# Maxima of the attention scores as two operand rows instead of a product of their own, another order of the lap, and zero fills moved one stage ahead

## The chip, the cores and the metric

One NeuronCore of a Trainium2 chip runs the whole program. The metric is the device time of one execution in microseconds; a profile is taken of one execution. PE is TensorE, DVE VectorE, ACT ScalarE, POOL GpSimd, SP the engine that here only issues DMAs. PE's granted clock is given as a share of 2.4 GHz.

## The reference

Two layers run over x of 32 sequences with 128 tokens of 128 channels. Each has a conditioning part and an expert part with eight experts, of which each token takes two. The change lies in the second layer's attention (16 heads, 8 channels each) and in the last steps of the first layer's experts:

```
q, k, v = split(layernorm(x) @ w_qkv + b_qkv)       # 16 heads of 8 channels
scores  = einsum('bqhd,bkhd->bhqk', q, k) / sqrt(8)
attn    = softmax(scores, axis=-1)                  # exp(score - maximum) / sum
x       = x + einsum('bhqk,bkhd->bqhd', attn, v) @ w_o + b_o
h       = layernorm(x)                              # then routing and experts
```

## The kernel before

The program is a row of stages, each a block in which all engines start together: layer 0 with its dispatch (to 106 us), its experts (`experts0`, to 237), conditioning and the q, k and v products (`pre_attention`, to 306), attention with norm, routing and dispatch of its result (`attention`, to 542), the second experts (`experts1`).

**Attention.** A lap `s` of 46 serves one sequence at each step of a software pipeline; four heads form a group g, 0 to 3. q and k are kept as a high and a low part, so that a product has 96 rows. PE computes the scores twice. `score(s + 2, g)` gives them with queries on the partitions, in ps1, against `km`, a k masked for each head by POOL (one head of four, `mask_k`) and ACT (three). From these DVE takes the negative maximum of each query (`maximum`, L1735, into `mneg`). `shift(s, g)` gives them with keys on the partitions, in ps2, against `qm`, a q masked by SP's loads from DRAM (`load_masked`, twelve DMAs for a pair of sequences), and adds the maxima; ACT then takes the exponent straight from ps2 (`exponent`, L1833). To bring the maxima into that layout POOL parts them into a high and a low piece (`part_max`, L1680 and L1682), PE turns them (`turn_max`, L1902), DVE spreads them over four masked blocks (`spread_max`, L1741, into `mxT`), and a second product with `selr` adds them in ps2 (L1896). ps1 and ps2 have two halves each, so a score waits for the maximum of two groups before, and a shift for the exponent of two groups before.

`mix` (L1914) multiplies the exponents with `vb`, the values spread by POOL (`spread_v`, L1690), `total` (L1923) sums them; DVE inverts and divides (`invert`, `divide`), `project` (L1933) applies w_o, and `keep` (L1756) adds the result to X3. From lap 6 on the group of four sequences that is done gets its norm, routing and dispatch in pieces, spread over four laps: moments and variance (lap 6), centring and turning (7), scaling and natural rows (8), routing (9), placing (10), where POOL also sends two pieces of rows in each lap (`post_scatter`, L358). In the text lap A is a lap with moments and placing, B the one with centring and turning, C with scaling, D with routing; they repeat.

The order is written out by hand for each engine. On PE a lap is four times score, shift, with `mix` behind the shift of g 0, `turn_max(s + 1)` behind that of g 1 (or 2), `project` behind that of g 2 (or 3), `total` behind that of g 3. SP loads the next pair's q and k (`load_pair`, three DMAs of 128 KB each), then the masked q, and in two pairs a fill.

**Fills.** The rows that experts read are written in the dispatch; regions of zeros are written before (`fill_region`, two DMAs of 1040 KB for each expert). Six of the eight regions of the second dispatch are filled in layer 0, two in attention. POOL waits for them in lap 10.

**End of the first experts.** SP loads rows and weights of each tile, then the modulations `eg` (L1007), then calls `fetch_halves`: V in four DMAs when the first sends are done, X3 in four when the second are (L865). DVE adds V to X (L956, needs all four), then two groups of X3 (L964), and the stage ends.

## Time and profile before

| | us |
|---|---|
| median of three runs (lowest, highest) | 696.9 (695.83, 698.49) |
| profiled execution: its time, its span | 700.72, 698.9 |
| PE, DVE, POOL, ACT busy, share of the span | 85%, 68%, 62%, 56% |
| mean granted clock of PE | 0.929 |

Starts of stages are read from the timeline, in us from the span's start. A duration of a matmul overlaps with the next one's, so what it costs in a row of such is the distance of two starts. A busy time by stretch counts overlapped parts once.

### The profile page before, as it was taken

To read this page: it belongs to the slowest core of one execution; us is meant where nothing else is said; L and a number is where in the kernel's file an instruction comes from. 1 tells how busy PE (TensorE), PEld (TensorE's weight loads), DVE (VectorE), ACT (ScalarE), POOL (GpSimd) and SP (SyncE) were. 2 spreads that over 40 slices of the span, in tenths; PEclk is the share of its full clock that TensorE was granted. 3 is DMA by queue.
4 is the path that set the end of the run, shared out by engine and by line. 5 is a ranking of instruction groups with operands and counts; after the bars stand their busy time and mean duration, and the time that the engine had idled before them with its cause. 6 is when DMAs were issued, how large, how long until landed. Compare 5 with 4: busy or idle time off the path is not lost.

```text
span 698.9 us, 17755 instructions
## 1 busy us (share of the span) xinstructions
PE 593.7 (85%) x5559; PEld 475.7 (68%) x5559; DVE 473.7 (68%) x1514; ACT 389.3 (56%) x841; POOL 433.3 (62%) x573
## 2 busy tenths in 40 slices
PE   4999953999998378869999999999961699999996
PEld 2566632988998256536766766766741599999993
DVE  3665552766777367756878788879745478888874
ACT  3544401655555068776777777778641355555551
POOL 2677760666677565534454878977777155666663
PEclk9999995999999589967999999999985699999999
DMA  7999996767677518561873443443113798888858
GB/s 224 249 203 297 288 260 145 196 205 198 202 224 226 202 39 247 205 203 55 251 202 87 111 125 105 127 126 85 47 36 98 220 300 269 251 249 252 246 186 267
DMA packets 106298, 131.23 MB, mean 188 GB/s; under 512 B 16272, under 2 KB 83888, under 8 KB 106096
## 3 DMA queue, kind: packets, MB, share of 16 engines
q1 hardware_dynamic: 92864, 109.40, 57.1%
q0 software_dynamic: 9088, 18.76, 8.2%
q10 hardware_dynamic: 4272, 2.14, 1.0%
q8 instruction: 39, 0.64, 0.4%
q14 instruction: 35, 0.29, 0.1%
HBM read 80.75 MB, written 49.50 MB: 186 GB/s over the span
## 4 chain that ended last, share of the span: by engine, by line
PE 29%; POOL 12%; issue 9%; DVE 2%; DMA 2%; ACT 1%; SPq 1%; ACTq 0%; POOLq 0%; DVEq 0%
PE psO L2058 10%; PE psA L939 8%; POOL late_rows L358 7%; PE ps L1884 2%; PE ps L1894 2%; PE ps L1896 2%; POOL vb L1690 2%; PE psAO L1914 2%; PE psAO L1923 1%; PE psT L889 1%; POOL X L1480 1%; POOL rstd L1473 1%; DMA kp<-qk_parts 1%; POOL xmx L1682 1%; SPq L1129 1%
## 5 line engine op out<-in xcount | busy, mean ns | idle before, releaser
L948 POOL DMA_INDIRECT expert_rows<-fo,to x78 | 84.6, 1085 | 62.5 <-DVE fo L2081 49.1
L1735 DVE TENSOR_REDUCE mneg<-ps 128x4 f32<-128x512 f32 x128 | 86.2, 676 | 41.4 <-PE ps L1884 39.9
L948 POOL DMA_INDIRECT expert_rows<-eo,to x78 | 75.1, 962 | 53.9 <-ACT eo L1094 34.2
L1833 ACT ACTIVATE arena<-ps 128x512 f32<-128x512 f32 x128 | 75.5, 590 | 49.8 <-PE ps L1896 48.8
L358 POOL DMA_INDIRECT dispatch_rows<-row,index x64 | 62.4, 976 | 34.4 <-issue 19.2
L921 DVE CAST xh<-psT 128x256 fp32r<-128x256 f32 x78 | 33.1, 424 | 66.6 <-PE psT L889 65.9
L358 POOL DMA_INDIRECT late_rows<-row,index x64 | 63.9, 998 | 20.3 <-issue 15.1
L939 PE MATMUL psA<-xh,wh 128*128 128x256 f32 (+1 forms) x234 | 73.3, 313 | 1.4 <-DVE xl L925 1.4
L1826 ACT ACTIVATE km<-kp,const 96x512 fp32r<-96x512 f32 x96 | 67.7, 712 | 3.4 <-PE ps L1884 1.3
L1884 PE MATMUL ps<-km,qp 96*128 96x512 f32 x128 | 63.4, 502 | 4.8 <-ACT km L1826 3.6
L939 PE MATMUL psA<-xh,wl 128*128 128x256 f32 (+1 forms) x234 | 66.9, 286 | 0.0
L939 PE MATMUL psA<-xl,wh 128*128 128x256 f32 (+1 forms) x234 | 66.7, 285 | 0.0
L1670 POOL TENSOR_SCALAR km<-kp,const 96x512 fp32r<-96x512 f32 x32 | 50.1, 1565 | 15.1 <-POOLq L1180 10.2
L2058 PE MATMUL psO<-wb,fh 128*128 128x128 f32 x464 | 56.4, 275 | 0.3 <-ACT fh L2140 0.3
L2058 PEld LDWEIGHTS psO<-wb,fh 128*128 128x128 f32 x464 | 54.3, 192 | 0.5 <-ACT fh L2140 0.5
L1894 PE MATMUL ps<-qm,kp 96*128 96x512 f32 x128 | 52.6, 411 | 0.9 <-DVE mxT L1741 0.5
L1896 PE MATMUL ps<-mxT,selr 128*128 128x512 f32 x128 | 51.7, 404 | 0.0
L939 PEld LDWEIGHTS psA<-xh,wh 128*128 128x128 f32 (+1 forms) x234 | 42.7, 182 | 2.3 <-DVE xl L925 2.2
L939 PEld LDWEIGHTS psA<-xl,wh 128*128 128x128 f32 (+1 forms) x234 | 42.8, 183 | 0.0
L939 PEld LDWEIGHTS psA<-xh,wl 128*128 128x128 f32 (+1 forms) x234 | 42.6, 182 | 0.0
L1884 PEld LDWEIGHTS ps<-km,qp 96*128 96x128 f32 x128 | 25.6, 201 | 19.4 <-issue 11.5
L2129 ACT ACTIVATE fw<-psO,xt 128x128 f32<-128x128 f32 x58 | 18.2, 365 | 33.7 <-PE psO L2058 27.2
(232 smaller groups left out, 1570.6 us busy)
## 6 DMA issues: line engine op xcount, KB each, us to landing
late_rows<-tail SPq DMA_DIRECT2D x17, 1040.0 KB, 18.4
wb<-in_W1b SPq DMA_DIRECT2D x29, 578.0 KB
w<-in_W SPq DMA_DIRECT2D x29, 304.0 KB
qk_parts<-qk SPq DMA_DIRECT2D x8, 1024.0 KB, 4.7
qp<-qk_parts SPq DMA_DIRECT2D x48, 128.0 KB
kp<-qk_parts SPq DMA_DIRECT2D x48, 128.0 KB
qm<-qk_parts SPq DMA_DIRECT2D x192, 32.0 KB
arena<-in_W1b SPq DMA_DIRECT2D x10, 578.0 KB
```

Source lines behind the costliest of these rows:

```text
L358: pool.indirect_dma_start(out=r.xbuf, out_offset=bass.IndirectOffsetOnAxis(ap=r.index[b][:, c:c + 1], axis=0), in_=r.row[b][:, c // TOPK, ...
L921: v.tensor_copy(z.xh[q][:], z.psT[:, q, 0:SLOTS]).then_inc(z.x_high, 1)
L939: ins = z.m.nc.tensor.matmul(out, w[k][q][:, columns], x[k][q][:], start=(k == 0), stop=(k == 2), skip_group_check=True)
L948: pool.indirect_dma_start(out=m.ybuf, out_offset=bass.IndirectOffsetOnAxis(ap=to[b][:, a:a + 1], axis=0), in_=out[b][:, a, :], in_offset=N ...
L1670: ins = nc.gpsimd.tensor_scalar(km[s % 2][:, :, j, :], kp[side(s)][:, :, tok(s)].bitcast(F32), mask(j), None, ALU.mult)
L1735: nc.vector.tensor_reduce(mneg[s % 2][:, g, :], ps1[:, g % 2, :].rearrange("p (j k) -> p j k", j=4), AX_X, ALU.max, negate=True).then_inc( ...
L1826: nc.scalar.activation(km[s % 2][:, :, j, :], kp[side(s)][:, :, tok(s)].bitcast(F32), ACT.Copy, scale=mask(j)).then_inc(km_act, 1)
L1833: nc.scalar.activation(prob[s % 2][:, g, :], ps2[:, g % 2, :], ACT.Exp, scale=ATT_SCALE).then_inc(exped, 1)
L1884: nc.tensor.matmul(ps1[:, g % 2, :], qp[side(s)][:, g, tok(s)], km[s % 2][:, g].rearrange("p j k -> p (j k)"), start=True, stop=True).then ...
L1894: nc.tensor.matmul(ps2[:, g % 2, :].rearrange("p (j k) -> p j k", j=4), kp[side(s)][:, g, tok(s)], qm[(s // 2) % 2][:, g, :, tok(s)], star ...
L1896: nc.tensor.matmul(ps2[:, g % 2, :], selr[:, g, :], mxT[s % 2][:].rearrange("p j k -> p (j k)"), start=False, stop=True).then_inc(shifted, 1)
L2058: ins = nc.tensor.matmul(psO[:, q, a * P:(a + 1) * P], h[q][:, k, a * P:(a + 1) * P], wb[b][:, WIDE + k * P:WIDE + (k + 1) * P], start=(k ...
```

## The change

The two pieces of the maxima become rows 96 and 97 of `qm`, against two rows of ones in `kp`, so that one product of 98 rows gives the shifted scores; L1896, `selr` and the spreading go. `mneg` is turned as it is (`turn_max` waits for DVE, not POOL), DVE parts the turned maxima with a copy and a subtraction (16 partitions, 128 columns), and SP sends each piece into its row of `qm` with a DMA of 8 KB (`send_max`); the shift waits for both (`max_landed`). `part_max` goes from POOL. The turned maxima and `project`'s result now lie in free columns of psAO instead of psM and psW, and the waits that guarded those two go. On PE `turn_max` stands at the head of the lap, `mix` behind the shift of g 1, `project` ahead of `total`; DVE's order follows. SP's list is written anew: k of pair k + 1, nine masked loads, the maxima of the even sequence, the last three masked loads, q of pair k + 2. The last two regions are filled in `experts0`, between `eg` and `fetch_halves`. In the diff the leading blanks of attention's lines are cut.

```diff
@@ -1006,6 +1004,8 @@
...
                         [DOWN, GT, 2 * P])).then_inc(m.gbu_in[b], 16)
+                for e in range(EARLY_FILLS, E):
+                    fill_region(m, sp, e)
                 fetch_halves(m, sp, st, 0)
...
@@ -1119,12 +1119,15 @@
...
+MAX_ROW = 96
...
-def load_pair(m, sp, n, b):
...
-    for side, parts in ((m.qp[b], (0, 1, 0)), (m.kp[b], (2, 2, 3))):
+def load_pair(m, sp, n, b, sides="qk"):
...
+    for name, side, parts in (("q", m.qp[b], (0, 1, 0)), ("k", m.kp[b], (2, 2, 3))):
+        if name not in sides:
+            continue
...
@@ -1229,7 +1232,7 @@
...
-                    nc.gpsimd.memset(m.qm[b][:].bitcast(F32), 0.0).then_inc(m.zeroed, 1)
+                    nc.gpsimd.memset(m.qm[b][0:MAX_ROW].bitcast(F32), 0.0).then_inc(m.zeroed, 1)
...
@@ -1575,11 +1578,12 @@
...
-    m.qp, m.kp = ([m.sb(f"{x}{b}", [96, HG, PAIR], F32R, ctx) for b in range(PAIR_BUFFERS)]
-                  for x in ("qp", "kp"))
+    m.qp = [m.sb(f"qp{b}", [96, HG, PAIR], F32R, ctx) for b in range(PAIR_BUFFERS)]
+    m.kp = [m.sb(f"kp{b}", [MAX_ROW + 2, HG, PAIR], F32R, ctx) for b in range(PAIR_BUFFERS)]
...
-    m.qm = [m.sb(f"qm{b}", [96, HG, 4, PAIR], F32R, ctx) for b in range(2)]
+    m.qm = [m.sb(f"qm{b}", [MAX_ROW + 2, HG, 4, PAIR], F32R, ctx) for b in range(2)]
...
+    m.max_in = m.sems("a_max_in0", "a_max_in1")
...
@@ -1594,11 +1598,31 @@
...
+def send_max(m, sp, s, rows, ready, shifted):
...
+    to, half = m.qm[(s // 2) % 2], slice((s % 2) * P, (s % 2 + 1) * P)
+    if s >= 4:
+        sp.wait_ge(shifted, HG * (s - 3))
+    for w in range(2):
+        sp.wait_ge(ready, 2 * s + w + 1)
+        sp.dma_start(to[MAX_ROW + w:MAX_ROW + w + 1, :, :, half].rearrange("o g j k -> o (g j) k").bitcast(F32),
+                     rows[:, w, :].bitcast(F32)).then_inc(m.max_in[s % 2], 16)
...
+def max_landed(engine, m, s):
...
+    engine.wait_ge(m.max_in[s % 2], 32 * (s // 2 + 1))
...
+MAXIMA, BY_WO = slice(2 * P, 3 * P), slice(3 * P, 4 * P)
...
@@ -1608,23 +1632,22 @@
...
-        selr = sb("selr", [P, HG, P], F32R)
...
-        xm = two("xmx", [P, 4, HG, 2])
-        mxT = two("mxT", [P, 4, P], F32R)
+        mxT = two("mxT", [HEADS, 2, P], F32R)
...
-        (cleared, made, km_pool, km_act, vb_done, scored, maxed, link, parted, turned, mxT_done, shifted,
+        cleared = m.zeroed
+        (made, km_pool, km_act, vb_done, scored, maxed, turned, mxT_done, shifted,
...
-            "a_cleared", "a_made", "a_km_pool", "a_km_act", "a_vb", "a_scored", "a_maxed", "a_link", "a_parted",
+            "a_made", "a_km_pool", "a_km_act", "a_vb", "a_scored", "a_maxed",
...
@@ -1642,19 +1665,26 @@
...
 def _(sp):
-    for k in range(PAIRS):
-        ahead = k + 1
-        if 2 <= ahead < PAIRS:
-            if ahead >= PAIR_BUFFERS:
-                sp.wait_ge(shifted, HG * 2 * (ahead - PAIR_BUFFERS + 1))
-            if ahead % 2 == 0:
-                sp.wait_ge(m.qk_out[ahead // 2 % 2], 16 * (ahead // 4 + 1))
-            load_pair(m, sp, ahead, ahead % PAIR_BUFFERS)
+    sp.wait_ge(m.qk_out[1], 16)
+    load_pair(m, sp, 2, 2)
+    send_max(m, sp, 0, mxT[0], mxT_done, shifted)
+    for k in range(1, PAIRS):
+        send_max(m, sp, 2 * k - 1, mxT[1], mxT_done, shifted)
+        if PAIR_BUFFERS <= k + 1 < PAIRS:
+            sp.wait_ge(shifted, HG * 2 * (k + 2 - PAIR_BUFFERS))
+            load_pair(m, sp, k + 1, (k + 1) % PAIR_BUFFERS, "k")
         if k >= 2:
             sp.wait_ge(shifted, HG * 2 * (k - 1))
-            load_masked(m, sp, k)
-        if k in (2, 3):
-            fill_region(m, sp, EARLY_FILLS + k - 2)
+            load_masked(m, sp, k, range(3))
+        send_max(m, sp, 2 * k, mxT[0], mxT_done, shifted)
+        if k >= 2:
+            load_masked(m, sp, k, (3,))
+        if k + 2 < PAIRS:
+            sp.wait_ge(scored, HG * 2 * (k + 3 - PAIR_BUFFERS))
+            if k % 2 == 0:
+                sp.wait_ge(m.qk_out[(k + 2) // 2 % 2], 16 * ((k + 2) // 4 + 1))
+            load_pair(m, sp, k + 2, (k + 2) % PAIR_BUFFERS, "q")
+    send_max(m, sp, SEQS - 1, mxT[1], mxT_done, shifted)
     sp.wait_ge(mixed, SEQS)
...
@@ -1667,19 +1697,9 @@
...
-            ins = nc.gpsimd.tensor_scalar(km[s % 2][:, :, j, :], kp[side(s)][:, :, tok(s)].bitcast(F32),
+            ins = nc.gpsimd.tensor_scalar(km[s % 2][:, :, j, :], kp[side(s)][0:96, :, tok(s)].bitcast(F32),
...
-    def part_max(s):
-        p = s % 2
-        pool.wait_ge(maxed, HG * (s + 1))
-        wait(pool, turned, s - 1)
-        hi, lo = (xm[p][:, :, :, w] for w in range(2))
-        mine = mneg[p][:].rearrange("p g j -> p j g")
-        nc.gpsimd.tensor_copy(hi.bitcast(F32R), mine).then_inc(link, 1)
-        pool.wait_ge(link, s + 1)
-        nc.gpsimd.tensor_tensor(lo, mine, hi, ALU.subtract).then_inc(parted, 1)
...
@@ -1693,10 +1713,6 @@
...
-        ins = nc.gpsimd.memset(mxT[b][:].rearrange("p j k -> p (j k)").bitcast(F32), 0.0)
-    ins.then_inc(cleared, 1)
-    part_max(0)
-    for b in range(2):
...
@@ -1704,8 +1720,6 @@
...
-        if s + 1 < SEQS:
-            part_max(s + 1)
...
@@ -1730,39 +1744,41 @@
...
-            wait(dve, parted, s - 1)
+            wait(dve, turned, s - 1)
...
-        wait(dve, shifted, HG * (s - 1))
-        nc.vector.tensor_tensor(mxT[s % 2][0:32], bc(psM[0:32, 0:P].unsqueeze(1), 32, 4, P),
-                                bc(m.const[0:32, C_MASK:C_MASK + 4].unsqueeze(2), 32, 4, P),
-                                ALU.mult).then_inc(mxT_done, 1)
+        if s >= 2:
+            max_landed(dve, m, s - 2)
+        hi, lo = (mxT[s % 2][:, w, :] for w in range(2))
+        mine = psO[0:HEADS, s % 2 ^ 1, MAXIMA]
+        nc.vector.tensor_copy(hi, mine).then_inc(mxT_done, 1)
+        dve.wait_ge(mxT_done, 2 * s + 1)
+        nc.vector.tensor_tensor(lo, mine, hi.bitcast(F32), ALU.subtract).then_inc(mxT_done, 1)
...
-        dve.wait_ge(made, s + 1)
+        dve.wait_ge(made, s + 2)
...
-        nc.vector.tensor_tensor(m.X3[:, s, :], psW[:, 0:P], m.X3[:, s, :], ALU.add).then_inc(kept, 1)
...
-    for g in range(HG):
-        ins = nc.vector.tensor_copy(selr[:, g, :], bc(m.const[:, C_SEL + g:C_SEL + g + 1], P, P))
-    ins.then_inc(cleared, 1)
+        nc.vector.tensor_tensor(m.X3[:, s, :], psO[:, s % 2, BY_WO], m.X3[:, s, :], ALU.add).then_inc(kept, 1)
...
+    for b in range(PAIR_BUFFERS):
+        ins = nc.vector.memset(kp[b][MAX_ROW:MAX_ROW + 2].bitcast(F32), 1.0)
+    ins.then_inc(made, 1)
...
-        if g == 2:
-            dve.wait_ge(cleared, 2)
+        if g == 1:
...
@@ -1770,36 +1786,35 @@
...
         varying, centring, routing, placing = (group(s, k) for k in (6, 7, 9, 10))
+        if s + 1 < SEQS:
+            spread_max(s + 1)
         if s + 2 < SEQS:
             maximum(s + 2, 0)
-        if varying is not None:
-            post_moments(post, dve, varying, kept)
         if centring is not None:
...
             post_logits(post, dve, routing, routing % 2, post.natural_banks)
+        if s + 2 < SEQS:
+            maximum(s + 2, 1)
         if inner:
             invert(s - 2)
-        if s + 2 < SEQS:
-            maximum(s + 2, 1)
+            divide(s - 2)
         if varying is not None:
-            post_gather(post, dve, varying)
+            post_moments(post, dve, varying, kept)
         if placing is not None:
             index_slot(r, dve, placing, post.rank_out)
-        if inner:
-            divide(s - 2)
         if routing is not None:
...
             maximum(s + 2, 2)
+        if varying is not None:
+            post_gather(post, dve, varying)
         if varying is not None:
...
             index_place(r, dve, placing, post.rank_out)
-        if s + 1 < SEQS:
-            spread_max(s + 1)
         if s + 2 < SEQS:
...
@@ -1889,17 +1904,14 @@
...
                 pe.wait_ge(qm_in[(s // 2) % 2], 16 * 12 * (s // 4 + 1))
-            pe.wait_ge(mxT_done, s + 1)
+            max_landed(pe, m, s)
         wait(pe, exped, HG * s + g - 1)
         nc.tensor.matmul(ps2[:, g % 2, :].rearrange("p (j k) -> p j k", j=4), kp[side(s)][:, g, tok(s)],
-                         qm[(s // 2) % 2][:, g, :, tok(s)], start=True, stop=False)
-        nc.tensor.matmul(ps2[:, g % 2, :], selr[:, g, :], mxT[s % 2][:].rearrange("p j k -> p (j k)"), start=False, stop=True
-                         ).then_inc(shifted, 1)
+                         qm[(s // 2) % 2][:, g, :, tok(s)], start=True, stop=True).then_inc(shifted, 1)
...
     def turn_max(s):
-        pe.wait_ge(parted, s + 1)
-        wait(pe, mxT_done, s)
-        nc.tensor.transpose(psM[0:32, 0:P], xm[s % 2][:].rearrange("p j g w -> p (j g w)"), m.ident
+        pe.wait_ge(maxed, HG * (s + 1))
+        nc.tensor.transpose(psO[0:HEADS, s % 2 ^ 1, MAXIMA], mneg[s % 2][:].rearrange("p g j -> p (g j)"), m.ident
                             ).then_inc(turned, 1)
...
@@ -1908,7 +1920,7 @@
...
-            wait(pe, divided, s - 1)
+            wait(pe, kept, s - 1)
...
@@ -1929,58 +1941,43 @@
...
         pe.wait_ge(divided, s + 1)
-        wait(pe, kept, s)
-        nc.tensor.matmul(psW[:, 0:P], oT[s % 2][:], m.wo[:], start=True, stop=True).then_inc(projected, 1)
+        nc.tensor.matmul(psO[:, s % 2, BY_WO], oT[s % 2][:], m.wo[:], start=True, stop=True).then_inc(projected, 1)
...
     score(1, 0)
+    turn_max(0)
     score(1, 1)
-    turn_max(0)
     score(1, 2)
-    pe.wait_ge(cleared, 3)
+    score(1, 3)
+    pe.wait_ge(made, 1)
     shift(0, 0)
-    score(1, 3)
     shift(0, 1)
...
         turning, scaling, routing, placing = (group(s, k) for k in (7, 8, 9, 10))
+        if s + 1 < SEQS:
+            turn_max(s + 1)
         for g in range(HG):
...
                 shift(s, g)
-            if behind and g == 0:
+            if behind and g == 1:
                 mix(s - 1, range(4))
+            if g == 3 and inner:
+                project(s - 2)
             if behind and g == 3:
...
             if g == 0 and placing is not None:
-                wait(pe, kept, min(s - 2, SEQS))
                 pe.wait_ge(post.nat_copied, placing + 1)
...
                 post_rank(post, pe, placing, placing % 2, post.rank_out)
-            if g == (1 if routing is None else 2) and s + 1 < SEQS:
-                if scaling is not None:
-                    pe.wait_ge(post.hT_done, scaling + 1)
-                if routing is not None:
-                    pe.wait_ge(post.nat_copied, routing + 1)
-                    pe.wait_ge(post.router.got, routing + 1)
-                turn_max(s + 1)
-            if g == (2 if routing is None and placing is None else 3) and inner:
-                if routing is not None:
-                    pe.wait_ge(post.nat_copied, routing + 1)
-                    pe.wait_ge(post.router.got, routing + 1)
-                if placing is not None:
-                    pe.wait_ge(post.router.slotted, placing + 1)
-                project(s - 2)
         if turning is not None:
-            wait(pe, mxT_done, min(s + 2, SEQS))
             wait(pe, post.nat_copied, turning)
...
         if scaling is not None:
-            wait(pe, kept, min(s - 1, SEQS))
-            wait(pe, mxT_done, min(s + 2, SEQS))
             wait(pe, post.router.slotted, scaling)
...
```

## Rows read from the trace of the kernel before

**Rows 1.** Busy time by stretch: length, then each engine's busy us (instructions), granted clock, DMA share, GB/s
```profile
314.26:322.56 8.30, 8.02 (x18) 4.84 (x18) 5.08 (x8) 4.46 (x8) 4.88 (x11) 0.50 0.01 2
322.56:502.25 179.69, 172.46 (x2432) 123.85 (x2431) 143.26 (x436) 134.91 (x254) 126.64 (x253) 1.00 0.47 128
```

**Rows 2.** Busy time of one lap without later work, columns as above
```profile
345.30:350.87 5.57, 5.57 (x80) 3.93 (x80) 4.45 (x9) 4.10 (x7) 3.33 (x8) 1.00 0.91 276
```

**Rows 3.** Timeline of PE: start, us, engine, line, out<-in, count
```profile
329.95 0.40 PE L1894 MATMUL ps<-qm,kp 96*128 96x512 f32 x1
330.19 0.40 PE L1896 MATMUL ps<-mxT,selr 128*128 128x512 f32 x1
330.42 0.27 PE L1902 MATMUL psM<-const,xmx 128*32 128x128 f32 x1
```

**Rows 4.** Busy time of one cycle of four laps
```profile
426.67:451.94 25.27, 24.02 (x343) 17.38 (x343) 20.62 (x70) 19.40 (x37) 20.86 (x39) 1.00 0.40 115
```

**Rows 5.** Timeline of PE; in brackets the idle time before and what ended it
```profile
314.26 0.76 PE L1894 MATMUL ps<-qm,kp 96*128 96x512 f32 x1 [0.48 <-DVE mxT L1741]
...
322.56 1.68 PE L1914 MATMUL psAO<-arena,vb 128*32 128x128 f32 x32
...
328.60 1.08 PE L1914 MATMUL psAO<-arena,vb 128*32 128x128 f32 x32
...
410.54 0.28 PE L1902 MATMUL psM<-const,xmx 128*32 128x128 f32 x1 [1.25 <-POOL xmx L1682]
```

**Rows 6.** Timeline of DVE at the end of the first expert stage
```profile
230.45 4.91 DVE L956 TENSOR_TENSOR X<-V,X 128x512 f32<-128x512 f32 x8 [2.93 <-DMA V<-expert_rows]
```

**Rows 7.** Part 6 of the page, DMA issues: KB each, median us to landing
```profile
late_rows<-tail SPq DMA_DIRECT2D x17, 1040.0 KB, 18.4
```

**Rows 8.** Timeline of SP's queue: start of the first issue, us until the last is issued
```profile
215.12 0.92 SPq L1007 DMA_DIRECT2D eg<-cond_rows  x2
...
412.47 1.69 SPq L1129 DMA_DIRECT2D qp<-qk_parts  x3
...
415.62 4.14 SPq L1594 DMA_DIRECT2D qm<-qk_parts  x12
```

**Rows 9.** Timeline of POOL, the mask of k in lap 7
```profile
359.34 1.57 POOL L1670 TENSOR_SCALAR km<-kp,const 96x512 fp32r<-96x512 f32 x1 [3.01 <-DMA kp<-qk_parts]
```

**Rows 10.** The chain of work that ended last, in order of time
```profile
353.41 5.84 DMA kp<-qk_parts
```

**Rows 11.** Busy time by stretch, columns as in rows 1
```profile
216.00:230.50 14.50, 9.87 (x83) 9.36 (x82) 8.83 (x24) 5.91 (x15) 11.14 (x12) 0.92 0.74 243
...
334.00:344.00 10.00, 10.00 (x149) 7.18 (x151) 8.59 (x16) 7.44 (x14) 4.17 (x12) 1.00 1.03 294
336.00:340.00 4.00, 4.00 (x57) 2.79 (x58) 3.17 (x7) 2.88 (x6) 1.43 (x3) 1.00 1.07 341
```

**Rows 12.** Timeline of POOL at the border of laps A and B
```profile
407.60 1.09 POOL L358 DMA_INDIRECT late_rows<-row,index  x1 [0.99 <-DVE index L339]
...
409.96 0.21 POOL L1680 CAST xmx<-mneg 128x16 fp32r<-128x16 f32 x1
...
410.47 1.57 POOL L1670 TENSOR_SCALAR km<-kp,const 96x512 fp32r<-96x512 f32 x1
```

**Rows 13.** Timeline of DVE: first maxima of laps B, D and A, and two others
```profile
407.24 0.27 DVE L1756 TENSOR_TENSOR X<-psW,X 128x128 f32<-128x128 f32 x1
407.43 0.67 DVE L1735 TENSOR_REDUCE mneg<-ps 128x4 f32<-128x512 f32 x1
...
420.83 0.69 DVE L1735 TENSOR_REDUCE mneg<-ps 128x4 f32<-128x512 f32 x1 [1.75 <-PE ps L1884]
...
424.90 0.66 DVE L1741 TENSOR_TENSOR mxT<-psM,const 32x512 fp32r<-32x512 f32 x1
...
426.67 0.67 DVE L1735 TENSOR_REDUCE mneg<-ps 128x4 f32<-128x512 f32 x1
```

**Rows 14.** DMA issues: KB each, us to landing
```profile
condT<-in_condT SPq DMA_DIRECT2D x1, 8.0 KB, 1.9
```

6 lines of the change are left out of this document (2 added, 4 removed).

## Prediction

> **What bounds the kernel now.** I read the busy times by stretch first. The attention stage from its second lap to the last scoring lap takes 179.69 us, and PE is busy for 172.46 of them at a granted clock of 1.00; before it stand 8.30 us at 0.50 [rows 1]. A lap is one sequence of 32. In the laps without later work PE has no gap: 5.57 us busy out of 5.57, DVE 4.45, ACT 4.10 [rows 2]. Each of the four maxima products (L1896) holds PE for 0.23 to 0.24 us, the distance from its start to the next start [rows 3]. From lap 6 on, four laps form a cycle, because the layer norm, routing and dispatch of a group of four sequences are spread over them. There are six of them up to about 502, and one is 25.27 us, from a block of value products to the fourth behind it. PE is busy for 24.02 us of it, DVE for 20.62, POOL for 20.86, ACT for 19.40 [rows 4]; the 1.25 that PE lacks is one wait of the turn of the maxima (L1902) for POOL [rows 5]. So PE bounds this stage, but by a small margin: whatever PE loses beyond about 3 us in a cycle meets the others.
>
> The other place that the change touches is the end of the first expert stage. There DVE stands idle for 2.93 us until the last quarter of V lands, and starts its eight additions at 230.45, 4.91 us long; the next stage can't start before they are done [rows 6]. V is on the path.
>
> **The change part by part.**
>
> *Fills into the first expert stage.* Four transfers of 1040 KB [rows 7], 4.26 MB, leave SP's queue in attention and enter it behind the loads of eg (issued from 215.12, two of them), ahead of V's fetches, which SP issues next [rows 8]. All of these are on one queue, and the trace shows that loads wait behind fills there: with the second pair of fills outstanding POOL waits 3.01 us for a kp [rows 9] whose transfer took 5.84 us on the chain [rows 10]; in the laps without fills no such wait appears. With fills and loads moving, the engines were full (share 1.03) at 294 GB/s over 10 us, at best 341 [rows 11]. 4.26 MB at these rates is 12.5 to 14.5 us. Between 216.0 and 230.5 the engines' share is 0.74 [rows 11], so 0.26 × 14.5 = 3.8 us is free for them; the rest, 8.7 to 10.7 us, pushes V back. DVE's additions, the next stage and all behind it follow one for one, as nothing else there is late. I take **+9.0**. Bounds: 6, if the fills go at the queue's best and use a gap behind 230 too; 12, if the rows that POOL sends out in the same stretch slow as well. The Trainium skill (DMA: Bandwidth & Descriptors, "Where 436 GB/s comes from") gives about 358 GB/s as what the memory side allows one core; its estimate would be 11.9 − 3.8 = 8.1 us, and the forecast 0.9 lower. In attention the fills leave nothing: the cycle in which POOL waited for kp is as long as the rest, and laps 2 to 5 are all 5.57 long although a fill falls into them. They come off at 0.
>
> *Maxima as two operand rows.* Removed from PE: four L1896 in a lap, 4 × 0.235 = 0.94 us; their weight loads ran beside other matmuls. Two more rows in the contraction (98 for 96) change nothing: the 128-row L1896 and the 96-row L1894 are equally far from their successors [rows 3]. Removed from POOL: part_max, 0.21 + 0.23 and gaps, 0.51 us from 409.96 to 410.47 [rows 12]. DVE loses L1741 (0.66) and gains a copy and a subtraction of 16x128 from PSUM. No row has that shape; the nearest reads 128 elements in each partition from PSUM too and takes 0.27 (L1756) [rows 13]. The second waits for the first, so 0.27 + 0.05 + 0.27 = 0.59. Between 0.3 saved in a lap, if 16 partitions are cheaper, and 0.1 lost, if the wait is 0.2, I take 0.07 saved.
>
> Added: two transfers of 8 KB in each lap, and a round trip. Turn, copy, subtraction: 0.3 + 0.27 + 0.05 + 0.27 + hand-overs = 1.1 us behind the lap's start; SP's issue 0.43 each; landing unknown. Bounds: 1.9, the landing of an 8 KB load [rows 14], and 5.84, a kp behind a full queue [rows 10]. As the queue in attention will be light without fills (115 GB/s in a cycle, share 0.40 [rows 4]), I take 2.2. The maxima are then there 1.1 + 0.43 + 2.2 = 3.7 us into the lap and wanted by the first shift of the next, 0.35 us into it: a lap of 3.4 us or more hides the trip. For every second sequence they queue on SP behind kp's three (1.4 to 1.7) and nine masked loads (9 × 0.345 = 3.1); then SP gets to them about 1.3 us after they are ready, and 4.7 us are needed, just the lap. SP itself: 4.14 for a pair's masked loads, 1.69 for qp's three, hardly more for kp's [rows 8], and 4 × 0.43 for the new ones: about 9.2 us, against 9.5 of two shortest laps. It fits without room, and the last three masked loads land about 0.3 us late in the shortest laps.
>
> *Order on PE.* turn_max moves from behind g 1 to the lap's head, the value products from g 0 to g 1, project to g 3. They issue the same instructions. But the turn now waits for the last maximum of the lap before, with only project and the sums (about 1.3 us) between its score and it, where two more groups lay between them. PE can no longer run ahead of DVE over a lap's border: every lap takes at least DVE's time. keep now stands ahead of the next value products as well, and is done a lap earlier, at no cost.
>
> *The laps.* PE needs 5.57 − 0.94 = 4.63, DVE 4.45 − 0.07; with hand-overs 4.75. Laps 2 to 5: 4 × 0.82 = **−3.3**; lap 1: **−0.9**; the laps behind the last cycle, in which PE has no scores left and two laps of shifts: **−1.0**.
>
> *A cycle, lap by lap.* Lap D (routing): DVE from its first maximum at 420.83 to that of the next lap at 426.67, 5.84 with hardly a gap; less 0.07, 5.77. Lap A (moments, placing): from 426.67 to 407.43 + 25.27 = 432.70, 6.03, less 0.07, 5.96 [rows 13]. PE's later work is 24.02 − 4 × 5.57 = 1.74 in a cycle; I split it by kind, 0.4 for the norm's transposes in B, 1.0 for the natural rows behind C, 0.3 for the rank in A. Lap B: PE 4.63 + 0.4 = 5.0; but POOL sends its two pieces behind A's index, 407.60 to 409.96, then masks k for 1.57 [rows 12], and the next lap's first score needs that: 0.9 + 0.3 + 2.4 + 1.6 = 5.2. Lap C: 4.63 + 1.0 = 5.6. Sum 22.5, with 0.3 for hand-overs **22.8**; 25.27 − 22.8 = 2.47, six times **−14.8**. Floor: PE alone 24.02 − 3.76 = 20.3, −30. Ceiling: hand-overs of 0.4 in each lap, 24.1, −7.
>
> *Start of attention.* The first shift (314.26 [rows 5]) waits for the maxima. Its mxT was written by 314.1; now two issues and a landing follow, 0.43 + 2.2, so **+2.7**; bounds 1 (the turn is a score earlier) and 6 (landing 5.84). The ones for kp's rows hide where the four L1759 casts stood.
>
> Sum: 9.0 + 2.7 − 0.9 − 3.3 − 1.0 − 14.8 = **−8.3 us**. The profiled execution took 700.7 us with a span of 698.9; it becomes 692.4. That execution stands 3.8 above the median of the three runs, 696.9, which becomes **688.6**.
>
> **The rivals.** (1) *The cycles gain little*: DVE's lap border costs 0.4 more in each lap. Attention gives 7 + 4.2 + 1.0 − 2.7, the fills take them: 696.9 − 9.5 + 9.0 = 696.4. For: A and D are full DVE laps. Against: DVE was idle for 25.27 − 20.62 = 4.6 us of a cycle. (2) *The fills are hidden*: V doesn't wait, because its pieces get their turn; 696.9 − 17.3 = 679.6. Against: the wait for kp [rows 9]. (3) *PE stays the bound* in cycles at about 21, 11 less than forecast: 678. (4) **Slower**: the maxima of every second sequence land late. Place: SP's queue, behind three kp and nine masked loads. Landing in 5.8 instead of 2.2, such a lap takes 1.1 + 0.43 + 5.8 − 0.35 = 7.0, its neighbour 4.9, on average 5.95; attention's laps average 179.69 / 30 = 6.0 now, so nothing is gained and the rest stands: 696.9 + 9.0 + 2.7 = 708.6. It decides from a landing of about 5.1 us, where mean laps of 5.6 just pay the fills. (5) *The clock*: waits in PE's first laps hold it at 0.50, where the stage starts now [rows 1]. At that level a block of 32 value products takes 1.68 instead of 1.08 [rows 5], 1.6 times as long; by that a lap of 4.75 is 3 us longer, and four more such laps make 701. The Trainium skill (TensorE: Matmul & The Clock Gate, "HAM oscillation") tells of waits for DMAs that bring the engine back to 1.2 GHz again and again; with waits here under 1 us I give it little, and its estimate in a lap would be the same 3 us.
>
> **How the numbers follow.** Forecast 0.45, with its own range 683 to 694; rival 1: 0.20; rivals 2 and 3: 0.15; rival 4: 0.14; rival 5: 0.06. The range 679 to 702 leaves out most of rival 4 and the fastest ends. About 0.5%, 3.5 us, is what a measurement tells from no change. Faster (under 693.4): 0.45 × 0.95 + 0.15 + a little of rival 1 = 0.61; within: 0.20; slower: 0.19.
>
> **What would show it.** V's wait on DVE ending at about 239 instead of 230.45. L1896 gone, PE's first shift at 317 plus the 9 of the fills. Blocks of value products 4.75 apart in laps 2 to 5 and 22.8 over a cycle, with PE idle before L1902 until DVE's maximum in laps D and A. If PE's first L1894 of a lap waits for a transfer of qm, rival 4 is at work; if DVE starts V's additions near 231, rival 2; if the clock's row is under 0.9 in attention, rival 5. Wrong would be above all the fill term, which rests on one queue keeping its order, and the landing, for which no row has the place.

## The result and the profile after

The changed kernel takes **703.2 us** (median of 20 runs, 699.4 to 706.5), the kernel before 696.4 in the runs beside it: a ratio of **1.0096**, interval 1.0077 to 1.0114. The forecast, 688.6 and faster, was wrong, and its range (679 to 702) missed by 1.2 us.

The profiled execution has a span of 700.7 us, only 1.8 above the one before, because the old profiled execution was itself 4 us slower than its kernel's median: there `eg` was issued at 215.12 [rows 8], here at 211.3, though the kernels don't differ up to that point. So the two traces are compared from the issue of `eg` on, by starts in their timelines:

| stretch, us | before | after | forecast |
|---|---|---|---|
| `eg` issued to first score | 93.1 | 102.1 | +9.0 |
| first score to first value products | 14.3 | 15.3 | +2.7 |
| laps 1 to 5 (value products 1 to 6) | 28.31 | 28.06 | -4.2 |
| laps 6 to 17 | 75.80 | 74.26 | -7.4 |
| laps 18 to 29 | 75.58 | 74.64 | -7.4 |
| laps 30 and 31 | 10.04 | 7.63 | -1.0 |
| rest | 186.6 | 187.4 | 0 |

The fills cost what was forecast and the start of attention less (1.0 for 2.7). The gain of the laps did not come: 5.1 us instead of 20.

Busy time by lap, in the columns of [rows 1]: first the kernel before (laps 18 to 21, cut from value products to value products, the cycle of [rows 4]; A, B, C and D as in the prediction), then the same laps after.

```profile
426.67:432.59 5.92, 5.92 (x95) 4.25 (x94) 5.92 (x26) 3.99 (x7) 3.81 (x9) 1.00 0.59 167
432.59:439.92 7.33, 6.08 (x84) 4.28 (x84) 4.82 (x11) 5.64 (x11) 6.18 (x11) 1.00 0.23 70
439.92:446.39 6.47, 6.47 (x88) 4.85 (x88) 4.45 (x9) 4.63 (x8) 5.88 (x11) 1.00 0.63 181
446.39:451.94 5.55, 5.55 (x80) 4.00 (x80) 5.43 (x27) 5.14 (x11) 5.00 (x10) 1.00 0.15 43
```
```profile
431.03:437.10 6.07, 4.66 (x77) 3.45 (x76) 5.92 (x26) 3.19 (x6) 2.08 (x4) 1.00 0.43 99
437.10:443.31 6.21, 5.53 (x80) 3.79 (x80) 4.54 (x11) 5.51 (x12) 5.39 (x9) 1.00 0.58 116
443.31:449.25 5.94, 5.80 (x85) 4.30 (x84) 4.11 (x10) 4.55 (x9) 5.41 (x9) 1.00 0.68 155
449.25:456.08 6.83, 5.74 (x90) 3.71 (x89) 6.70 (x29) 5.59 (x13) 6.32 (x13) 1.00 0.44 113
```

PE did get lighter: 21.73 us in the cycle instead of 24.02. But the cycle is 25.05 for 25.27. Read the fourth number, DVE: in A it was busy for all 5.92 us before, beside a PE that was busy for the same 5.92. B lost 1.12 us (the wait for POOL [rows 5] is gone), C 0.53; A and D grew by 0.15 and 1.28, with DVE at 5.92 of 6.07 and 6.70 of 6.83.

A part of D's growth is only where the cut falls. The value products now stand a group later, and so five of DVE's maxima fall between D's two cuts instead of four, and four between B's instead of five. The prediction cut A and D at DVE's first maximum of a lap. Cut so, before and then after:

```profile
426.67:432.72 6.05, 6.05 (x98) 4.38 (x101) 6.05 (x27) 3.99 (x7) 3.81 (x9) 1.00 0.58 165
432.72:439.65 6.93, 5.68 (x83) 4.15 (x79) 4.42 (x11) 5.64 (x11) 5.91 (x11) 1.00 0.20 62
439.65:446.11 6.46, 6.46 (x89) 4.85 (x87) 4.43 (x9) 4.63 (x8) 5.87 (x11) 1.00 0.63 182
446.11:451.93 5.82, 5.82 (x81) 4.00 (x79) 5.70 (x27) 5.14 (x11) 5.27 (x10) 1.00 0.18 52
```
```profile
430.21:436.74 6.53, 5.12 (x89) 3.89 (x86) 6.36 (x28) 3.51 (x7) 2.54 (x7) 1.00 0.37 87
436.74:442.80 6.06, 5.38 (x80) 3.64 (x79) 4.39 (x12) 5.53 (x11) 5.24 (x9) 1.00 0.60 120
442.80:448.95 6.15, 6.01 (x86) 4.45 (x84) 4.32 (x11) 4.54 (x9) 5.62 (x9) 1.00 0.64 151
448.95:455.22 6.27, 5.18 (x81) 3.22 (x80) 6.20 (x28) 5.13 (x11) 5.76 (x9) 1.00 0.51 124
```

A and D grew by 0.48 and 0.45, and DVE fills them but for 0.17 and 0.07 us; B and C fell by 0.87 and 0.31.

The lap borders after, in the timeline (start, us, operation, in brackets the idle time before it and its releaser): D into A, A into B, B into C.

```profile
428.48 0.54 DVE L292 TENSOR_TENSOR diff<-best 128x4 f32<-128x4 f32 x1
429.38 0.39 DVE L303 TENSOR_TENSOR mask<-hot 128x32 bf16<-128x32 f32 x1
429.70 0.27 DVE L1758 CAST mxT<-psAO 16x128 fp32r<-16x128 f32 x1
430.03 0.17 PE L264 MATMUL psW<-mask,tri 128*128 128x8 bf16 x1 [0.49 <-DVE mask L303]
430.21 0.67 DVE L1749 TENSOR_REDUCE mneg<-ps 128x4 f32<-128x512 f32 x1
...
435.17 0.68 DVE L1749 TENSOR_REDUCE mneg<-ps 128x4 f32<-128x512 f32 x1
435.90 0.28 PE L1914 MATMUL psAO<-const,mneg 128*16 128x128 f32 x1 [1.41 <-DVE mneg L1749]
437.08 0.51 SPq L1609 DMA_DIRECT2D qm<-mxT  x1
...
441.95 0.27 PE L1914 MATMUL psAO<-const,mneg 128*16 128x128 f32 x1
442.26 0.28 DVE L1758 CAST mxT<-psAO 16x128 fp32r<-16x128 f32 x1 [1.60 <-PE psAO L1914]
```

At A's end PE stands 1.41 us before the turn (L1914) for DVE's last maximum; at the ends of B and C DVE stands 1.60 and 1.76 us for the turn, which PE reaches only behind its sums. Each engine waits for the other, in different laps. At D's end DVE finishes the choices before it parts the maxima; two of these small steps took 0.54 and 0.39 us (in the old cycle the same lines took 0.14 and 0.17 on average), and PE's rank product waits for the last. They are slow in four of the six cycles (0.19 and 0.17 us in the first, 0.16 and 0.18 in the last); why isn't settled. DVE's cycle is 21.27 us instead of 20.62: what the parting saves (0.55 for 0.67, four times) those two steps lose again, and some 0.5 us more is spread over many steps and isn't explained.

At the stage before:

```profile
212.25 7.94 SPq L409 DMA_DIRECT2D late_rows<-tail  x4
236.94 0.69 DVE L954 TENSOR_TENSOR X<-V,X 128x512 f32<-128x512 f32 x1 [9.64 <-DMA V<-expert_rows]
```
```profile
236.00:240.00 4.00, 0.00 (x0) 0.00 (x0) 3.06 (x6) 0.00 (x0) 0.00 (x0) 0.50 1.01 390
240.00:244.00 4.00, 0.21 (x1) 0.24 (x2) 3.25 (x7) 0.00 (x0) 0.40 (x1) 0.50 0.20 82
```

DVE waits 9.64 us for V where it waited 2.93 [rows 6], `eg` to V's addition is 25.6 us for 15.3, and the DMA engines, full until 240, are idle right behind.

### The profile page after: what moved, and what is told of

It is laid out like the page before. It is cut to its first block, busy times and chain, and to the rows that moved or that the text cites. A ratio compares the mean times of both kernels' runs of the same rounds, so it can differ in the third digit from the quotient of the medians.

```text
span 700.7 us, 17432 instructions
## 1 busy us (share of the span) xinstructions
PE 574.7 (82%) x5431; PEld 460.2 (66%) x5431; DVE 477.2 (68%) x1545; ACT 387.4 (55%) x841; POOL 419.5 (60%) x507
## 3 DMA queue, kind: packets, MB, share of 16 engines
q10 hardware_dynamic: 4272, 2.14, 1.0%
## 4 chain that ended last, share of the span: by engine, by line
PE 24%; POOL 14%; issue 10%; DVE 2%; DMA 2%; SPq 1%; ACT 1%; ACTq 0%; POOLq 0%
PE psO L2055 10%; PE psA L937 8%; POOL late_rows L356 7%; POOL km L1700 4%; POOL vb L1710 2%; PE psT L887 1%; PE ps L1899 1%; PE ps L1909 1%; POOL rstd L1476 1%; POOL X L1483 1%; DVE mneg L1749 1%; PE psAO L1926 1%; DMA qm<-qk_parts 1%; SPq L1598 1%; ACTq L2153 0%
## 5 line engine op out<-in xcount | busy, mean ns | idle before, releaser
L1749 DVE TENSOR_REDUCE mneg<-ps 128x4 f32<-128x512 f32 x128 | 84.3, 678 | 7.1 <-PE ps L1899 6.9
L356 POOL DMA_INDIRECT late_rows<-row,index x64 | 63.8, 997 | 17.3 <-issue 15.3
L1899 PE MATMUL ps<-km,qp 96*128 96x512 f32 x128 | 60.1, 475 | 6.4 <-ACT km L1841 3.9
L1909 PE MATMUL ps<-qm,kp 98*128 98x512 f32 x128 | 54.7, 432 | 11.2 <-ACT arena L1848 5.1
L1909 PEld LDWEIGHTS ps<-qm,kp 98*128 98x128 f32 x128 | 24.9, 196 | 24.1 <-ACT arena L1848 13.8
L1899 PEld LDWEIGHTS ps<-km,qp 96*128 96x128 f32 x128 | 25.5, 200 | 20.1 <-issue 9.8
```

The costliest lines, as they stand in the source:

```text
L356: pool.indirect_dma_start(out=r.xbuf, out_offset=bass.IndirectOffsetOnAxis(ap=r.index[b][:, c:c + 1], axis=0), in_=r.row[b][:, c // TOPK, ...
L1749: nc.vector.tensor_reduce(mneg[s % 2][:, g, :], ps1[:, g % 2, :].rearrange("p (j k) -> p j k", j=4), AX_X, ALU.max, negate=True).then_inc( ...
L1899: nc.tensor.matmul(ps1[:, g % 2, :], qp[side(s)][:, g, tok(s)], km[s % 2][:, g].rearrange("p j k -> p (j k)"), start=True, stop=True).then ...
L1909: nc.tensor.matmul(ps2[:, g % 2, :].rearrange("p (j k) -> p j k", j=4), kp[side(s)][:, g, tok(s)], qm[(s // 2) % 2][:, g, :, tok(s)], star ...
```

## The experiments

Ratios are to the kernel before, in runs on the same chip, with 95% intervals; the changed kernel's own is 1.0096. "Cycle" is a third of laps 18 to 29 unless single laps are named. Edits are against the changed kernel unless said otherwise. The chips' own times differ (696 to 705 us for the kernel before, 768 on one, called the slow chip below), so only ratios and stretches are compared. Ratios of two kernels whose intervals overlap don't tell the two apart, and single laps vary between the cycles of one kernel.

### The fills

**Moved alone, and put back alone.**

```diff
 # b1_fills_moved: the kernel before
+                for e in range(EARLY_FILLS, E):      # experts0, behind eg
+                    fill_region(m, sp, e)
-                    if k in (2, 3):                  # attention
-                        fill_region(m, sp, EARLY_FILLS + k - 2)
 # a1_fills_back: the changed kernel, the same reversed, behind load_masked(m, sp, k, (3,))
```

> The kernel before with one edit: the four zero fills of the last two regions are issued in the first expert stage, as the changed kernel has them, and no longer in the attention. Theory (the prediction's): they stand ahead of the fetch of V and of the normalised rows and cost about 9 us (6 to 12): 705 us where the kernel before has 696.4. Rival one: they are hidden in transfers that wait anyway: 696 us. Rival two: they cost 9 us here but the attention's early laps win back what the fills cost them there, 3 us or more: 702 us or less.

> The changed kernel with the four fills back in the attention's list of SP, behind the loads of the third and fourth pair. Theory: the fills cost the changed kernel what they were forecast to, so this gives 694 us against its 703.2. Rival one, fills without effect: 703 us. Rival two: 4.2 MB of fills beside the maxima's DMAs and the operands' loads stall the early laps by 3 to 5 us, so this gives 698 us.

Moved alone: 1.0072 (1.0041 to 1.0103), some 5 us, where the theory had 9; by rows `eg` to first score grew by 8.4. Laps 1 to 17 took the same 104.1 us as with the fills in them, but that is a balance: lap 7, in which POOL no longer waits 3.01 us for its keys [rows 9], takes 6.22 us for 7.09, and lap 1 takes 6.98 for 6.05, at a clock of 0.74 for 0.89. So in the old order the fills cost lap 7 some 0.9 us; that its cycle is as long as the rest says nothing, as it has no placing in it. The prediction's term for the first expert stage holds by rows. Back alone: 1.0068 (1.0041 to 1.0096), by the ratios 2 us better than the changed kernel, which the intervals don't separate. `eg` to V is 15.8 us again, but laps 1 to 5 take 33.3 for 28.1 and laps 6 to 17 79.3 for 74.3: **the new order has no cover for them.** That is rival two of the run, twice over: a part of it is clock, 0.69 to 0.92 in laps 3 to 7, where the changed kernel has 1.00, and a lap's first shift waits for the maxima, 8 KB behind 1040 KB:

```profile
355.18 0.50 PE L1909 MATMUL ps<-qm,kp 98*128 98x512 f32 x1 [3.45 <-DMA qm<-mxT]
```

**On ScalarE's queue**, same bytes, one in each of laps 3 to 6 instead of two in laps 3 and 5 (`fill_region(m, act, ...)` behind the last exponent of s = 3 to 6).

> The changed kernel with its four fills issued by ScalarE's queue, one behind the last exponent of laps 4 to 7 of the attention, instead of by SP ahead of the fetch. In the attention on SP's queue they made laps 1 to 18 10.2 us longer (33.3 and 79.3 for 28.1 and 74.3). If it is the queue (the maxima, keys and masked queries of 4 to 128 KB wait behind fills of 1040 KB), laps 1 to 18 grow by 3 us at most here, the step from the expert stage to V is 15.5 us again, and the kernel has a ratio of 0.995 to the kernel before. If it is their bytes, laps 1 to 18 grow by 8 us or more and the ratio is 1.005 or more.

1.0065 (1.0042 to 1.0088). Laps 1 to 17 take 110.0 us for 102.3: 7.7 of the 10.2 us stay. ScalarE spent 0.38 to 0.44 us on each issue. So most of it comes with the fills on either queue, and the place in SP's list is the smaller part; the fall of the clock to 0.82 and 0.74 in laps 3 and 4 is in it. The shift of lap 3, which waits 1.81 us in the changed kernel, here waits 4.67:

```profile
344.64 0.79 PE L1909 MATMUL ps<-qm,kp 98*128 98x512 f32 x1 [4.67 <-DMA qm<-qk_parts]
```

**With SP's order of loads changed as well**: `load_masked(m, sp, k, range(3))` ahead of `load_pair(..., "k")`.

> The same with SP's loads of three heads of masked queries ahead of the next pair's keys. If the laps of 6.9 and 6.5 us among the first five are the place of the masked queries on SP, they fall to 5.5 or less and laps 1 to 6 from 28.1 to 26 us. If the keys are then late instead, other laps grow by as much and the kernel is within 1 us of the other.

1.050 (1.047 to 1.054), laps 1 to 5 39.4 us, cycles 29.6: masks of k wait 7.5 and 13.0 us for their keys. Both loads sit at their deadline: with these two exchanged the keys are the late ones.

```profile
357.96 1.56 POOL L1698 TENSOR_SCALAR km<-kp,const 96x512 fp32r<-96x512 f32 x1 [13.02 <-DMA kp<-qk_parts]
```

**Behind the fetch** (the two lines of `experts0` below `fetch_halves`).

> The changed kernel with its four fills issued behind the fetch of V and of the normalised rows instead of ahead of it. In the trace after, the DMA engines stand at 0.00 to 0.20 of their time from 240 to 264 us, right behind the fetch, and the step from the expert's last loads to V's first use has grown from 15.3 to 25.6 us. Theory: the fills' whole cost is their place ahead of the fetch, so this gives that step back (15.5 us again) and 8 to 10 us in all: a ratio to the kernel before of 0.996 to 0.999. Rival, the bytes collide with the next block's first loads behind the fetch: half of it comes back, a ratio of 1.003.

0.9976 (0.9936 to 1.0016), on the slow chip: by the ratios about 8 us better than the changed kernel. Four more kernels below hold this edit, on another chip: `eg` to V is 14.9 to 16.1 us in them, and `eg` to first score 95.8 to 99.5, for 102.1 after and 93.1 before. About half of that stretch comes back, as the rival had it. DVE is done with the stage as early as before, but SP is busy with the four fills for 11.1 to 11.5 us and starts the next stage's loads 26.5 to 27.8 us behind `eg`, for 22.4 before and 32.3 after. The DMA engines are still full there, so those loads collide with the fills as well:

```profile
230.84 11.31 SPq L409 DMA_DIRECT2D late_rows<-tail  x4
240.00:244.00 4.00, 1.09 (x4) 0.71 (x4) 0.00 (x0) 0.00 (x0) 1.37 (x3) 0.50 1.10 336
```

In this one (a17) the next stage starts 4.7 us later than before and the first score comes 2.7 later, so there the collision adds nothing to the delay by the issues; how it shares in the others isn't separated.

### The laps

**TensorE lighter in the old order** (the kernel before; leaves out the shift by the maximum, with the exponent's scale at 0.001).

```diff
-                                     ..., start=True, stop=False)
-                    nc.tensor.matmul(ps2[:, g % 2, :], selr[:, g, :], mxT[s % 2]..., start=False, stop=True
-                                     ).then_inc(shifted, 1)
+                                     ..., start=True, stop=True).then_inc(shifted, 1)
```

> The kernel before without the second product of each shift (the one that adds the maxima by the selecting rows); the maxima are still found, parted, turned and spread. Left out so: the shift by the maximum; the exponent's scale is 0.001 instead of 0.354 so that nothing overflows. What the forecast counted on alone, in the old order: 0.39 us less of TensorE four times a lap. Theory of the forecast (TensorE bounds the cycle, 24.0 us of 25.2): a cycle falls by 3.7 us at least, to 21.5 or to VectorE's 20.6, the kernel by 25 us or more. Rival (TensorE is busy, and is not what sets the lap; the ring TensorE, VectorE and back through the scores' two banks is): a cycle falls by less than 1.5 us, the kernel by less than 10.

0.9903 (0.9885 to 0.9921), 6.8 us. Laps 14 to 17, A to D:

```profile
392.54:398.60 6.06, 5.62 (x91) 3.48 (x90) 6.06 (x27) 4.14 (x9) 4.95 (x10) 1.00 0.69 175
398.60:405.54 6.94, 5.20 (x81) 3.53 (x80) 4.84 (x13) 5.64 (x11) 5.72 (x10) 1.00 0.27 75
405.54:411.60 6.06, 6.01 (x85) 4.00 (x84) 4.42 (x9) 4.54 (x8) 5.31 (x10) 1.00 0.64 187
411.60:416.76 5.16, 5.07 (x76) 3.31 (x75) 5.16 (x24) 4.93 (x11) 4.90 (x10) 1.00 0.23 69
```

The cycle falls by 1.0 us, to 24.2, though four products a lap are gone. In A and D DVE is busy for the whole lap (6.06 of 6.06, 5.16 of 5.16; cut at the first maxima 6.05 of 6.05 and 5.59 of 5.59). The rival holds. The theory's 3.7 us a cycle is more than the prediction had: that put A and D at DVE's time itself (5.96 and 5.77), and was off here in B (5.2 for 6.94, with POOL's parting still waited for) and C (5.6 for 6.06, with PE busy for 6.01). From lap 19 on B takes 8.3 to 8.5 us instead of 6.9:

```profile
427.00:428.00 1.00, 1.00 (x17) 0.64 (x19) 1.00 (x2) 0.93 (x3) 1.00 (x3) 1.00 0.00 0
428.00:429.00 1.00, 1.00 (x28) 0.85 (x20) 0.91 (x3) 1.00 (x3) 0.83 (x4) 0.50 0.18 35
430.00:431.00 1.00, 1.00 (x4) 0.48 (x2) 0.11 (x1) 0.00 (x0) 1.00 (x2) 0.50 0.97 275
```

PE had waited 1.72 us for POOL at 426.28, and its granted clock falls to the lower level (1.2 GHz) until 431. That costs 1.4 us a cycle in the last three. The same wait of 1.74 us at 377.88 and 402.08 left the clock at 1.00, so the wait alone doesn't decide it; what does, these rows don't show.

**One engine lighter at a time in the new order.**

```diff
 # a4_no_remainder: DVE; the low part of the maxima is left out (sent as zeros)
-                    nc.vector.tensor_tensor(lo, mine, hi.bitcast(F32), ALU.subtract).then_inc(mxT_done, 1)
 # a5_short_totals: PE; four of sixteen products of total, with a tile of ones
+                    for g in range(HG):
+                        ins = nc.tensor.matmul(..., ones[:], prob[p][:, g, 0:P], start=True, stop=True)
 # a6_less_act: ScalarE; one of three copies of mask_k, exponent's scale 0.001
+                    if s > 2 and j == 3:
+                        return
```

> The changed kernel without the second parting operation (the remainder lo, 0.28 us on VectorE with the wait for hi ahead of it); its row is sent as zeros. Left out: the maxima's low part. If VectorE's own work is what sets the laps, each lap falls by 0.3 to 0.4 us, a cycle by 1.2 to 1.6, the kernel by 10 us. If only the ring at the lap border counts, the same, since both operations stand between the turn and the first maximum. If TensorE or ScalarE sets the laps: within 2 us of the changed kernel.

> The changed kernel with four of the sixteen products that sum the exponents (12 x 0.07 us of TensorE less a lap). Left out: twelve of sixteen heads' own sums. If TensorE sets the laps, a cycle falls by 3.3 us. If the ring at the lap border does (last maximum, sums, turn, parting, first score, first maximum), the sums stand in it: VectorE's idle 1.6 us before its parting goes in the two light laps, a cycle falls by 1.5 to 3 us. If VectorE's work in the two heavy laps or ScalarE sets the laps: less than 1 us a cycle.

> The changed kernel with one of ScalarE's three masked copies of k left out from the fourth sequence on (0.71 us of ScalarE a lap; exponent's scale 0.001 so that nothing overflows). Left out: the last head of each group scores against old keys. If ScalarE sets part of the laps (copies that stand ahead of exponents, exponents that TensorE's shifts wait for, 0.8 us a cycle in the trace), a cycle falls by 1 us or more, the kernel by 7. Otherwise within 2 us of the changed kernel.

| laps, us | A | B | C | D | ratio |
|---|---|---|---|---|---|
| after | 6.07 | 6.21 | 5.94 | 6.83 | 1.0096 |
| DVE lighter (22 to 25) | 6.07 | 6.09 | 5.92 | 6.48 | 1.0074 |
| PE lighter (14 to 17) | 6.26 | 6.21 | 5.28 | 8.02 | 1.0095 |
| ScalarE lighter (22 to 25) | 6.08 | 6.01 | 5.93 | 6.46 | 1.0076 |

By the ratios none is worth over 2 us to the kernel, where 7 us and more were the price if its engine set the laps (intervals 1.0052 to 1.0096, 1.0077 to 1.0114, 1.0046 to 1.0106), and the laps answer differently: C to PE alone (-0.66, with PE at 5.80 of 5.94 after) and B to ScalarE (-0.20) hold in most cycles. B's -0.12 and D's -0.35 are from undisturbed ones: with DVE lighter, D is up to 7.15, and laps 15 and 16 are 7.33 and 7.08; with ScalarE lighter, D is up to 6.99. A answers to none: DVE's 0.28 us less leave it at 6.07. PE's relief is again paid in clock: 0.87 over its D, 0.75 over its A.

```profile
419.82:425.10 5.28, 5.15 (x61) 3.64 (x60) 4.10 (x10) 4.53 (x9) 4.74 (x8) 1.00 0.38 119
425.10:433.12 8.02, 5.92 (x67) 3.43 (x66) 6.26 (x29) 6.04 (x13) 7.13 (x13) 0.87 0.53 125
```

**The value products first again** (`if behind and g == 0`).

> The changed kernel with the value products back behind the first score and shift instead of behind the second. Theory: this order matters little, since TensorE has 3.3 us of idle time in a cycle of 25.05: within 1.5 us of 703.2. Rival: the products at the second place delay the exponents behind them or the first score's successor delays the maxima; then this order is worth 0.3 us a lap either way, 694 us or 713 us.

1.0323 (1.0294 to 1.0351), cycle 27.5: 0.7 us a lap on average, most of it in A (7.6 to 8.1 for 6.07). In A DVE waits 0.9 to 1.1 us for a score behind the products and PE then 1.57 for the last maximum: with the turn at the head, the products between the scores delay the maximum that the turn needs. My "no matter" was wrong; this part of the change is needed by the other.

**The turn later**, behind the lap's first score and shift, alone and with SP's four heads issued together (a16, with the fills behind the fetch).

```diff
 # a3_turn_later
+                        if g == 0 and s + 1 < SEQS:
+                            turn_max(s + 1)            # PE, behind shift(s, 0); DVE: spread_max behind maximum(s + 2, 0)
 # a16_later_heads, SP
-                        load_masked(m, sp, k, range(3))
+                        load_masked(m, sp, k)
```

> The changed kernel with the maxima's turn put behind the first score and first shift of its lap instead of ahead of them, and VectorE's two parting operations behind that lap's first maximum. Theory: the turn at the head of the lap ties TensorE to VectorE's last maximum of the lap before; in the trace after TensorE idles 1.4 us there once a cycle and VectorE then idles 1.6 us in each of the next two laps, so with the turn later a cycle falls by 1.0 to 1.5 us and the whole by 6 to 9 us: 696 us. Rival one, what binds is VectorE's work in the two laps with the router's steps, whatever the turn does: 702 to 703 us. Rival two, the later turn makes the maxima land too late for the shift of the next lap, and the cycles grow: 706 us.

> The kernel with the fills behind the fetch and the turn of the maxima behind the first score and shift, and with all four heads of masked queries issued on SP ahead of the maxima of the pair's first sequence (before: three heads, the maxima, the fourth). If the later turn failed by SP's list (the fourth head waits for maxima that come 1 us later, and the shift waits for it), the lap that took 7.1 to 7.8 us falls to 6.5 or less and cycles to 24.5 or less. If the later turn fails by itself (the maxima's own way to the shift), cycles stay at 26 or more.

a3: 1.0222 (1.0189 to 1.0255); a16: 1.0077 (1.0040 to 1.0114). A and B (laps 22 and 23) of a3, then A, B and C of a16:

```profile
471.91:477.46 5.55, 4.79 (x76) 3.29 (x75) 5.48 (x24) 3.72 (x7) 1.36 (x2) 1.00 0.38 99
477.46:485.52 8.06, 5.83 (x81) 3.73 (x80) 4.91 (x13) 5.35 (x11) 7.21 (x10) 1.00 0.61 119
```
```profile
459.56:465.12 5.56, 4.81 (x76) 3.30 (x76) 5.49 (x24) 3.73 (x7) 1.37 (x2) 1.00 0.37 97
465.12:471.83 6.71, 5.55 (x80) 3.72 (x79) 4.51 (x12) 5.34 (x11) 5.90 (x9) 1.00 0.49 134
471.83:477.83 6.00, 5.99 (x84) 4.22 (x83) 4.31 (x11) 4.54 (x9) 5.45 (x9) 1.00 0.41 112
```

A falls by 0.5 us in both, as the tie at its end says. But cycles are 26.0 and 25.3. In a3 the shift waits up to 1.84 us for masked queries (1.46 in a cycle): SP holds the fourth head back behind maxima that now come later. With the four heads together that wait is gone, and now the shift waits for the maxima themselves, in two early laps (2.14 and 1.62 us) and in some later ones (up to 0.92). 25.3 lies between a16's two expectations: SP's list was somewhat over half of a3's loss (0.73 of 1.16 us a cycle). The rest stays with the later turn, and B costs 0.5 more than with the turn at the head; there PE waits 0.84 us for exponents, for 0.47. As far as these runs go, the trip over SP and DMA holds the turn at the head, and the tie in A is its price. The theory that a later turn would win 6 to 9 us fell.

**What stands ahead of the turn, moved** (both with the fills behind the fetch): the stream's turns to the next lap's first group on PE (a17); `choose_hot` and `choose_mask` ahead of `maximum(s + 2, 3)` on DVE (a18); both (a19); and the placing one lap later (a15).

> The kernel with the fills behind the fetch, and with the four turns of the normalised stream (0.46 us on TensorE and a wait for ScalarE's norm) moved from the end of their lap, ahead of the maxima's turn, to the next lap behind the first score and shift. Theory (the lap's head is a meeting of TensorE and VectorE): lap B falls by 0.4 to 0.6 us, the next gains none of it back beyond 0.1, a cycle falls by 0.4 to 0.6 and the kernel by 3 us against the fills behind alone. Rival (B is set by ScalarE, busy 5.51 of 6.21 us): B stays within 0.2.

> The kernel with the fills behind the fetch, and with the router's last choices and mask on VectorE (0.9 us once a cycle) ahead of the lap's last maximum instead of behind it, so that the parting of the maxima and the next first maximum follow at once. Theory: in lap D the first maximum no longer waits 1.3 us behind them and TensorE's rank product no longer waits for the mask; but the turn comes later: D falls from 6.8 to 6.3 at best, a cycle by 0.5. Rival (VectorE's work of D, 6.70 us, is the lap, in whatever order): D stays within 0.2.

> The last two edits together. If the laps are closed one by one, the gains add: a cycle 0.8 to 1.1 us below 25.05, the kernel at a ratio of 0.989 to the kernel before. If a gain in one lap is a loss in the next, less than the better of the two.

> The kernel with the fills behind the fetch, and with the router's placing of each group (the rank product on TensorE, three index steps of 1.3 us on VectorE, the scatters on GpSimd) one lap later, so that it no longer shares a lap with the variances; the last group keeps its lap. Theory (the cycle is the sum of four laps of which VectorE fills two, 5.92 of 6.07 and 6.70 of 6.83 us): the lap of 6.07 falls to 5.2 or less, the next grows by 0.3 at most, a cycle falls by 0.6 to 1.2 us, the kernel by 4 to 7 us against the fills behind alone. Rival (another chain sets that lap, VectorE merely fills it): no lap changes by over 0.2 us, the kernel stays.

a17: 1.0008 (0.9977 to 1.0038). C falls by 0.4 to 5.55, B grows by as much to 6.66; there PE waits 0.73 us for ScalarE's copy of k, ScalarE being busy for 5.98:

```profile
461.01:467.67 6.66, 5.49 (x81) 3.78 (x80) 4.90 (x12) 5.98 (x13) 5.80 (x10) 1.00 0.47 121
467.67:473.22 5.55, 5.55 (x85) 4.36 (x84) 3.90 (x9) 4.08 (x8) 5.05 (x9) 1.00 0.55 140
```

a18: 1.0065 (1.0032 to 1.0097), D 7.2 to 7.4 with a wait of 1.3 to 1.4 before the turn: the work is only moved to the other side of the meeting, and now PE waits for it. a19: 1.0051 (1.0025 to 1.0078), the two do not add. a15: 0.9993 (0.9954 to 1.0031) on the slow chip, beside 0.9976 of the fills alone. Where D didn't spill over (laps 10 and 14) A is 5.92 and 6.01 instead of 6.07, not the 5.2 expected; later A is 6.5 to 6.9. DVE sat idle for 3.0 us ahead of D, waiting for the turn. A relief behind a wait isn't used: my theory of this run fell too.

**Pair loads on ScalarE** (q and k, six DMAs in two laps).

> The kernel with the fills behind the fetch, and with the attention's pair loads of q and k (six DMAs in two laps) issued by ScalarE instead of SP. SP issues for some 11.5 of 12.4 us in two laps of the trace after. Theory A (SP's list is a bound: late masked queries in the early laps, 0.4 us a cycle later on): 4 us less than with the fills behind alone, all of it in the first six laps (28.1 to 24.5 us), cycles 24.9 to 24.5. Theory B (VectorE's two full laps and the turn at the lap's head bound the cycle): cycles stay at 24.7 to 25.0. Rival: six issues on ScalarE cost it 2 us in two laps, and its exponents come later: cycles 25.5 or more.

1.013 (1.008 to 1.018), on the slow chip: A and B as before (6.1 and 6.2), the early laps too (28.2), C 7 to 11 us. Theory A fell for the early laps, and the run's rival (cycles of 25.5 or more) came true at 27.4. In C PE waits up to 2.5 us for exponents, and the clock is 0.69 to 0.84 in some; which comes first isn't settled, and on that chip other kernels' laps are disturbed too.

One more run (a12) had the later turn as well. If only SP's list had spoilt it, cycles of 23.5 to 24.2 were expected, else 25.5 or more. It took 1.0111 (1.0046 to 1.0177) with cycles of 27.1, and C laps of up to 9.8 us as in a11, so it doesn't separate the two.

## Why the prediction was wrong

- **Fills, +9.0**: right by rows, +9.0 from `eg` to the first score, and V's wait ended 10.3 us later. Moved alone it timed 5 us (3 to 7), less. "In attention the fills leave nothing" was 0.9 us off in lap 7 of the old order; in the new order they cost 10 us. I didn't ask what cover the new order leaves.
- **Start of attention, +2.7**: +2.0 to the first shift and 1.1 less behind it, +1.0 in all, the lower bound. Over-priced.
- **Lap 1, -0.9**: -0.6. **Laps 2 to 5, -3.3**: +0.4. Two laps do take 4.71 and 4.52 us, as priced at 4.75, but two others 6.90 and 6.52, where the shift waits 1.81 and 1.48 us for masked queries:

```profile
344.83 0.50 PE L1909 MATMUL ps<-qm,kp 98*128 98x512 f32 x1 [1.81 <-DMA qm<-qk_parts]
```

  I had SP's list at 9.2 us of 9.5 and wrote "It fits without room". From one pair's keys to the next it took 10.6 and 11.5 us, with hardly a gap: keys 2.3 and 2.6 where I had hardly more than 1.7, and 0.57 a send for 0.43:

```profile
334.72 2.34 SPq L1132 DMA_DIRECT2D kp<-qk_parts  x3
345.29 2.61 SPq L1132 DMA_DIRECT2D kp<-qk_parts  x3
356.75 1.53 SPq L1132 DMA_DIRECT2D kp<-qk_parts  x3
```

  It is rival 4's place with another load: not the maxima came late, but what queues beside them. (With the fills behind the fetch a lap of 6.9 to 7.9 remains there, and a part of it is clock, 0.76 to 0.96 in it and the one behind.)
- **A cycle, -2.47, the step that failed**: -0.4 on average (-2.5 over six). The sum of 22.5 was 25.0, and every term was too small. Cut at the first maxima, as I had cut A and D: A 5.96 forecast and 6.53 measured, **B 5.2 and 6.06**, C 5.6 and 6.15, D 5.77 and 6.27. For A and D I took DVE's time in the old order, less 0.07; in the new order DVE is busy for 6.36 and 6.20 of them, by the slower small steps and by growths that aren't explained. For B I priced PE and POOL and left out ScalarE (5.64 in the old B, 5.53 in the new one) and the turn behind it. For C I split too little of PE's later work to it (PE is busy for 5.80 to 6.01). The 0.3 for hand-overs was the measure of a tie that costs about 1 us a cycle, by a sum and not by a run: the largest busy times of the laps add up to 5.92 + 5.53 + 5.80 + 6.70 = 23.95 by the first cut (24.1 by the second), and the cycle is 25.05. My sentence that PE can no longer run ahead of DVE was right and stood there without a price.
- **Rival 1** is what happened in mechanism; I gave it 0.20 and under two thirds of its size (7.8 us lost in the cycles, where 12.3 were). Its argument against, DVE's 4.6 idle us in a cycle, was the error in small: that idle time lay in B and C, and DVE has it there still, waiting for the turn.
- **Rival 5**: in the traces of the changed kernel the clock stays at 1.00 through the cycles. But it was close: both kernels with less work on PE lost it in cycles, and so did several with PE's work unchanged (DVE lighter, the choices first, the value products first). The Trainium skill (TensorE: Matmul & The Clock Gate, "A second HAM failure mode: psum-queue depth-cycling") tells of a kernel where "the PE micro-idles between MM groups frequently enough that HAM oscillates"; the rows agree in part: 0.50 for some 3 us behind a wait of 1.72, at 1.4 us a cycle, but 1.00 behind the same wait in two cycles of the same kernel, and behind the 1.25 in the kernel before [rows 5].
- Sum by rows: 9.0 + 1.0 - 0.6 + 0.4 - 2.5 - 2.4 + 0.8 = 5.7 us, with 6.8 measured.

No version here that computes everything beats the kernel before beyond its interval. The best, the changed kernel with the fills behind the fetch (0.9976 and, with one more neutral edit, 1.0008), is level with it: the 4 us that attention gains (5.1 in the laps less 1.0 at its start) are about what the fills still cost (2.7 to 6.4 us from `eg` to the first score).

## What to carry to other kernels

Take the bound lap by lap, and for every engine in each lap: idle time of an engine in one lap is no slack for its work in another when something ties the two. Cut laps at the same operation before and after, and look which work the cut moves from one lap to the next. Where a change adds a point at which two engines wait for each other in every iteration, price it as the sum over the iterations of the larger of the two, plus the hand-over. A transfer that is free beside old code has to be priced again beside new waits: ask which DMA the new order puts on the path, and what is in front of it.

## What the runs showed of the hardware

- Fills of 1040 KB on another engine's queue still delayed the loads of 32 KB (a wait of 4.67 us where 1.81 stood without them) and made 17 laps 7.7 us longer, on the same queue 10.2. In these two runs the second queue gave little protection.
- An issue of such a fill took ScalarE 0.38 to 0.44 us in attention; four on SP took 7.9 us in the expert stage, and 11.1 to 11.5 us behind its last fetches, where the next stage's start waited for them.
- The granted clock fell to the lower level in spells in the middle of a stage in both kernels whose only change was less work for PE (laps of 8.3 us for 6.9), and in some with PE's work unchanged (0.97 and 0.76 in laps 13 and 14 with the choices first). The same wait of 1.7 us went with such a spell in three cycles of one kernel and with none in two.
